# Top-k attention on Trainium2: a penalty moved to GpSimd and the programs of four engines put in another order

## The reference

```python
scores = jnp.einsum('bhnd,bhmd->bhnm', q, k) * DHEAD ** (-0.5)
kth = jax.lax.top_k(scores, TOPK)[0][..., -1:]
masked = jnp.where(scores >= kth, scores, jnp.finfo(scores.dtype).min)
attn = jax.nn.softmax(masked, axis=-1)
o = jnp.einsum('bhnm,bhmd->bhnd', attn, v)
```

## Time and profile before

| What | Value |
|---|---|
| Median of 3 runs | 5586.61 us (5582.31 to 5589.42) |
| The profiled execution, its own time | 5584.55 us |
| Its span, first to last instruction | 5582.5 us |
| Top-k stage, first to last hand-on (L667) | 139.2 to 3348.1 us |
| TensorE matmuls busy | 4367.2 us (78%) |
| VectorE busy | 4406.7 us (79%) |
| ScalarE busy | 4164.0 us (75%) |
| GpSimd busy | 1502.2 us (27%) |
| Mean granted TensorE clock | 0.832 of full speed |

### The profile page before, as it was taken

One profiled execution on the slowest core, in us unless ns is written; L12 is line 12 of the kernel. 1 busy time (PEld: TensorE's weight loads), 2 busy tenths in 40 slices (PEclk: granted clock), 3 DMA queues, 4 the chain that ended last, 5 costly groups with the idle time before them and its releaser, 6 DMA issues. The chain is left out here.

```text
span 5582.5 us, 114219 instructions
## 1 busy us (share of the span) xinstructions
PE 4367.2 (78%) x32459; PEld 2805.0 (50%) x32459; DVE 4406.7 (79%) x25684; ACT 4164.0 (75%) x6084; POOL 1502.2 (27%) x362
## 2 busy tenths in 40 slices
PE   7575677766777477677777678988999999999998
PEld 4443445544544244445544454445655655655655
DVE  4999999989999999999999993224777777777775
ACT  2786799988988589889998893433666766666664
POOL 0443444444544244444554440010000000000000
PEclk8777677777777677777777779989999999999999
DMA  5000000000000000000000001014010010010012
GB/s 198 6 17 14 7 17 17 9 14 17 16 8 16 5 16 17 15 7 17 17 7 17 16 16 44 8 40 158 22 29 21 22 30 21 21 30 21 22 30 86
DMA packets 79607, 154.88 MB, mean 28 GB/s; under 512 B 8120, under 2 KB 49464, under 8 KB 73528
## 3 DMA queue, kind: packets, MB, share of 16 engines
q1 hardware_dynamic: 78904, 146.72, 9.3%
HBM read 99.50 MB, written 47.19 MB: 26 GB/s over the span
## 5 line engine op out<-in xcount | busy, mean ns | idle before, releaser
L539 POOL TENSOR_TENSOR a_probs<-a_scores,a_probs 128x2304 f32<-128x2304 f32 x288 | 1460.3, 5090 | 1778.2 <-ACT a_probs L462 1778.2
L557 DVE MAX8 a_top<-a_scores 128x8 f32<-128x36 f32 x18432 | 1831.2, 180 | 46.4 <-ACT a_scores L446 45.7
L373 PE MATMUL a_ps_t<-ident,a_probs 128*128 128x128 f32 x5184 | 976.2, 326 | 702.5 <-ACT a_probs_t L457 570.8
L373 PEld LDWEIGHTS a_ps_t<-ident,a_probs 128*128 128x128 f32 x5184 | 675.5, 164 | 989.4 <-ACT a_probs_t L457 707.5
L1110 PE MATMUL b_ps_t<-ident,b_soft 128*128 128x128 f32 x5184 | 794.3, 286 | 97.9 <-ACT b_soft_t L1183 69.6
L462 ACT ACTIVATE a_probs<-a_scores,a_steep_kth 128x2304 f32<-128x2304 f32 x290 | 641.2, 2211 | 294.7 <-DVE a_minus_max L667 294.7
L1195 DVE TENSOR_SCALAR_CACHE_REDUCE b_soft<-b_ps_s 128x2304 f32<-128x2304 f32 x290 | 741.7, 2558 | 86.9 <-PE b_ps_s L1097 67.3
L1183 ACT ACTIVATE b_soft_t<-b_ps_t 128x512 f32<-128x512 f32 (+1 forms) x864 | 438.0, 525 | 473.2 <-PE b_ps_t L1110 472.5
L1110 PEld LDWEIGHTS b_ps_t<-ident,b_soft 128*128 128x128 f32 x5184 | 557.6, 142 | 450.8 <-issue 304.2
L457 ACT ACTIVATE a_probs_t<-a_ps_t 128x512 f32<-128x512 f32 (+1 forms) x1440 | 726.8, 545 | 20.7 <-PE a_ps_t L373 7.2
L1168 ACT ACTIVATE b_soft<-b_soft,b_minus_max 128x2304 f32<-128x2304 f32 x289 | 642.1, 2222 | 30.2 <-issue 16.8
(11 more groups left out here) (127 smaller groups left out, 4279.6 us busy)
## 6 DMA issues: line engine op xcount, KB each, us to landing
a_k_stack<-k_parts SPq DMA_DIRECT2D x72, 288.0 KB, 6.0
b_k_stack<-k_parts SPq DMA_DIRECT2D x72, 288.0 KB, 6.1
a_q_ring<-q_parts SPq DMA_DIRECT2D x294, 64.0 KB
b_q_ring<-q_parts SPq DMA_DIRECT2D x294, 64.0 KB
k_parts<-p_high SPq DMA_DIRECT2D x36, 256.0 KB, 2.1
k_parts<-p_rest SPq DMA_DIRECT2D x36, 256.0 KB, 2.2
q_parts<-p_high SPq DMA_DIRECT2D x36, 256.0 KB, 2.0
q_parts<-p_rest SPq DMA_DIRECT2D x36, 256.0 KB, 2.0
```

What stands on the lines that cost most here:

```text
L373: last = pe.transpose(ps_t[(NTG * s + g) % 2][:, P * m:P * m + P], probs[s % 2][:, P * (m0 + m):P * (m0 + m) + P], cst["ident"][:, :])
L539: pool.tensor_tensor(probs[u][:, :], scores_all[:, 2 * (p % 2) + u, :], probs[u][:, :], ALU.subtract).then_inc(masked_ready, 1)
L557: last = dve.max(top8[s // 2 % 2][:, s % 2, c, :], scores_all[:, s % 4, CHUNK * c:CHUNK * c + CHUNK])
```

## The change

GpSimd makes the first tile's penalty itself: a tensor_scalar writes 3e38 where the score is below the 64th value and 0 elsewhere, from a new small tile `kept_kth`, and its subtraction follows. ScalarE makes the second tile's penalty only, as the last step of its pair. ScalarE's pair begins with `keep_scores` of the pair two ahead, which now waits until GpSimd has read the slot. TensorE's order follows; `weigh` of the second tile's last groups and `add_quadrants` move into the next pair. On VectorE `select` comes ahead of all chunks of the next pair, the last part of it (`pick`) after chunk 23 and `hand_on` after chunk 47. TensorE's and ScalarE's loops run 7 times from pair 2 on, with pairs before and after written out; GpSimd's first head is written out.

```diff
@@ TensorE @@
+            def pair_step(p, h):
+                pair = h * HEAD_PAIRS + p
+                here, before, after = exists(pair), exists(pair - 1), exists(pair + 1)
+                if exists(pair + 2):
+                    score(p + 2, 0, h)
+                if before:
+                    for g in range(2, NTG):
+                        weigh(p - 1, 1, g, h)
+                if exists(pair + 2):
+                    score(p + 2, 1, h)
+                if here:
+                    for g in range(3):
+                        turn(p, 0, g, h)
+                if before:
+                    pe.wait_ge(parts_ready, pair)
+                if after:
+                    count_doubts(pair + 1)
+                if here:
+                    turn(p, 0, 3, h)
+                    turn(p, 0, 4, h)
+                if after:
+                    pe.wait_ge(any_ready, pair + 2)
+                if before:
+                    add_quadrants(pair - 1)
+                    pe.wait_ge(o_kept, pair)
+                if here:
...
+                    for g in range(NTG):
+                        weigh(p, 0, g, h)
+                    for g in range(3):
+                        turn(p, 1, g, h)
+                    weigh(p, 1, 0, h)
+                    turn(p, 1, 3, h)
+                    turn(p, 1, 4, h)
+                    weigh(p, 1, 1, h)
+
+            for p in range(-2, 2):
+                pair_step(p, 0)
+            with pe.Fori(0, HEADS - 1) as h:
+                for p in range(2, HEAD_PAIRS + 2):
+                    pair_step(p, h)
+            for p in range(2, HEAD_PAIRS + 1):
+                pair_step(p, HEADS - 1)
...
@@ ScalarE @@
+                if exists(pair - 2):
+                    act.wait_ge(masked_ready, tile - 3)
+                act.activation(scores_all[:, 2 * (p % 2) + u, :], ps_s[:, 0:N], ACT.Copy).then_inc(scores_kept, 1)
...
+                if second:
+                    keep_scores(p + 2, 0, h)
+                if here:
+                    exponentials(p, 0, h)
+                    keep_turned(p, 0, 0, h)
+                if before:
+                    keep_parts(pair - 1)
+                if here:
+                    keep_turned(p, 0, 1, h)
+                    keep_turned(p, 0, 2, h)
+                if after:
                     keep_any(pair + 1)
...
+                if second:
+                    keep_scores(p + 2, 1, h)
+                if here:
+                    keep_turned(p, 0, 3, h)
+                if before:
+                    finish(p - 1, h)
+                if here:
+                    keep_turned(p, 0, 4, h)
+                    exponentials(p, 1, h)
+                if second:
+                    guess_place(p + 2, 0, h)
+                if here:
+                    for g in range(4):
+                        keep_turned(p, 1, g, h)
+                if second:
+                    guess_place(p + 2, 1, h)
+                if here:
+                    keep_turned(p, 1, 4, h)
+                if after:
+                    penalty(p + 1, 1, h)
...
@@ GpSimd @@
+                if u == 0:
+                    if not first:
+                        wait_alone(pool, turned, pair * (2 * NTG) - NTG)
+                    wait_alone(pool, kth_ready, pair + 1)
+                    pool.tensor_scalar(probs[0][:, :], scores_all[:, 2 * parity, :], kept_kth[parity][:, 0:1], -LOWEST,
+                                       ALU.is_lt, ALU.mult).then_inc(first_penalty, 1)
+                    pool.wait_ge(first_penalty, pair + 1)
+                else:
+                    pool.wait_ge(penalty_ready, pair + 1)
+                pool.tensor_tensor(probs[u][:, :], scores_all[:, 2 * parity + u, :], probs[u][:, :],
+                                   ALU.subtract).then_inc(masked_ready, 1)
...
@@ VectorE @@
+                return found
+
+            def pick(found):
                 for u in range(2):
                     after(found[u])
...
                 dve.tensor_scalar(steep_kth[parity][:, :], kth[:, :], STEEP, None, ALU.mult)
+                dve.tensor_scalar(kept_kth[parity][:, :], kth[:, :], 1.0, None, ALU.mult)
...
+                found = select(pair - 1, top8[(p - 1) % 2]) if before else None
+
                 def between(c):
-                    if c == 7 and before:
-                        select(pair - 1, top8[(p - 1) % 2])
-                    if c == 19 and before:
+                    if c == 23 and before:
+                        pick(found)
+                    if c == 47 and before:
                         hand_on(pair - 1, (p - 1) % 2)
```

More of the change, by code:

```diff
@@ L303, in attention_top @@
         minus_max = [sb(f"minus_max{n}", [P, 2]) for n in range(2)]
+        kept_kth = [sb(f"kept_kth{n}", [P, 2]) for n in range(2)]
         above = sb("above", [P, 1])
@@ L321, in attention_top, with exists @@
         HEAD_PAIRS = B * PAIRS
+        def exists(pair):
+            return not isinstance(pair, int) or 0 <= pair < ALL_PAIRS
         block = ctx.enter_context(nc.Block())
@@ L403, in add_quadrants @@
                 last.then_inc(added, 1)
-            score(0, 0, 0, first=True)
-            for s in range(1, 5):
-                score(s, 0, s)
-            count_doubts(0)
-            with pe.Fori(0, HEADS) as h:
-                for p in range(HEAD_PAIRS):
-                    pair, tile = h * HEAD_PAIRS + p, h * HEAD_TILES + 2 * p
-                    s = 2 * p
-                    pe.wait_ge(probs_ready, tile + 1)
-                    turn(s, 0, tile)
-                    turn(s, 1, tile)
-                    score(s + 5, h, tile + 5)
+            def pair_step(p, h):
[24 more added lines that the diff above has]
+                if here:
@@ L452, in exponentials, with keep_turned @@
+            def exponentials(p, u, h):
+                ahead, of_head = divmod(p, HEAD_PAIRS)
+                act.wait_ge(masked_ready, h * HEAD_TILES + 2 * p + u + 1)
+                act.activation(probs[u][:, :], probs[u][:, :], ACT.Exp, scale=SCALE,
+                               bias=minus_max[p % 2][:, u:u + 1], accum_out=sums[:, 2 * of_head + u, cols(h + ahead, 1)]
                                ).then_inc(probs_ready, 1)
-            def keep_turned(s, g, tile):
+            def keep_turned(p, u, g, h):
@@ L487, in finish @@
+            def finish(p, h):
+                ahead, of_head = divmod(p, HEAD_PAIRS)
+                act.wait_ge(added, h * HEAD_PAIRS + p + 1)
+                act.activation(o_all[:, 2 * of_head:2 * of_head + 2, cols((h + ahead) * D, D)],
                                ps_o[:, O_COL:O_COL + 2 * D].rearrange("p (u d) -> p u d", d=D),
                                ACT.Copy).then_inc(o_kept, 1)
-            for s in range(4):
-                keep_scores(s, s)
-            for u in range(2):
-                guess_place(u, 0, 0)
@@ new lines, in pair_step @@
+            def pair_step(p, h):
+                pair = h * HEAD_PAIRS + p
+                here, before, after, second = exists(pair), exists(pair - 1), exists(pair + 1), exists(pair + 2)
+                if second:
[9 more added lines that the diff above has]
+                if after:
+                    keep_any(pair + 1)
+                if second:
[18 more added lines that the diff above has]
+                    penalty(p + 1, 1, h)
@@ L526, in _ @@
+            for p in range(-2, 2):
+                pair_step(p, 0)
+            with act.Fori(0, HEADS - 1) as h:
+                for p in range(2, HEAD_PAIRS + 2):
+                    pair_step(p, h)
+            for p in range(2, HEAD_PAIRS + 1):
+                pair_step(p, HEADS - 1)
         @block.gpsimd
```

165 lines of the change are left out of this document (55 added, 110 removed).

## The result

The changed kernel takes **6740.84 us** (median of 4 runs, 6737.73 to 6748.61), the kernel before 5585.26 us beside it (4 runs). The ratio is 1.207, with a 95% interval of 1.205 to 1.2091. Forecast were 5539 us and a range up to 5670, so the sign and the size were both wrong. The profiled execution took 6748.61 us, its span is 6746.8.

The account below looks back on a forecast made before the run. It took a ring through VectorE, ScalarE and GpSimd as the bound, 20.6 us a plain pair; 20.3 after the change, 0.34 less times 143, gave -48 us from 5584.55: 5537, plus 2.1, 5539 us; range 5470 to 5670.

Parts of the forecast that it names:

- The tensor_scalar (x): GpSimd's added 128x2304 tensor_scalar ahead of its first subtraction: taken as 2.8 us, costing nothing until about 4.
- a late GpSimd blocks select: First subtraction still runs when VectorE starts select, whose first operation must wait; decides from x = 4; 5724 us, chance 0.20.
- S + 16.2 + x: Start of the next select when GpSimd is late, S being this select's start; 21.6 us a pair with x = 5.4.
- The port: VectorE and GpSimd excluding each other on SBUF: GpSimd's second subtraction against select's last operands, taken to add zero.
- margin of 0.2: Second subtraction starts about S + 2.1, S being select's start; select reads its last two-input operands at S + 1.96.
- The failed margin: GpSimd's second subtraction gets in ahead of select's last operands: up to +700 us, above 6200, chance 0.04.
- The row of 0.29 us: Trace row: select's first operation took 0.29 us beside a GpSimd copy and ended with it; elsewhere it takes 0.17.
- VectorE's own pair: VectorE's work from one select start through chunks, pick, hand-on and prepare: 19.76 us if nothing is late.
- The recounts: 19 recounts in VectorE's top-k stage, 8.0 us each over a plain pair, 152 us together, kept unchanged.
- The rival of a slow TensorE: ScalarE's wait for TensorE sets the period: 20.8 us a pair if TensorE stays at low clock, 5608 us, chance 0.17.
- Its counterargument: At the low clock TensorE is almost always busy, and the mean of 0.75 says it always returned to 2.4 GHz.
- Loop-backs: Seven loop-backs of ScalarE, 2.56 us each, 17.9 together, left as they are, between -18 and +18.

Follow-up runs that it names:

- prices by themselves: Kernel before with a block in front timing GpSimd forms over 128x2304 alone, then eight small VectorE operations begun during GpSimd subtractions; the change's tensor_scalar took 8.04 us.
- x = 6.10: Changed kernel with GpSimd's tensor_scalar doing the comparison alone, the multiplication by 3e38 left out: 6465.6 us.
- x = 2.11: Changed kernel with GpSimd's tensor_scalar writing a constant by mult and add, the comparison left out: 5570.76 us.
- a pair of edits that each read as "no use": Kernel before with first penalty and first subtraction in two pieces, and a pair's finish moved behind the next first exponential: both 0.9947, finish alone 1.002, pieces alone 1.0022.

## Why the prediction was wrong

**The tensor_scalar (x): the step that failed first.** The prediction took 2.8 us and 2.7 to 5.4 as bounds. It is 8.04. The low end rested on a COPY as "the only wide one-input row"; the run with prices by themselves has 2.10 for the copy and 6.10 with one comparison, so the kind of operation mattered more than the number of inputs. The high end took the subtraction's rate as that of a slow instruction; with two operations the rate is 8.04 / 2304 = 3.49 ns a column, where the subtraction has 2.2. An upper bound had to stand above it: the only tensor_scalar in the trace, 602 ns for 128 columns, allowed for up to 4.7 ns a column, or 10.8 us, and was discounted as fixed cost on no row's evidence. The prediction's two estimates, 2.0 and 3.9 us, came from the Trainium skill, GPSIMD Engine Reference: 1.03 cycles per element stands under Performance versus the Vector engine, the 2.03 of compare bodies under Performance pitfalls for Q7 kernels and not where the prediction puts it. The measured 6.04 to 8.05 us disagree with both.

**The rival "a late GpSimd blocks select" was the mechanism,** with its price formula right. S + 16.2 + x with x = 8.04 is 24.24 a pair, (24.24 - 20.64) x 143 = 515, or 6100 us. The run with the second subtraction held back, in which only this block exists, took 6094.4, with pairs of 24.15 to 24.45. By the formula the block at x = 6.10 should be 1.94 shorter than at 8.04; `factor` was 1.88 shorter.

**The port: the step that failed second.** "I take zero" with a margin of 0.2 us was worked out for a `select` that starts on time. In that case the second subtraction starts when ScalarE's penalty ends, just behind `select`'s last operand. When the first subtraction is late, the second's penalty is already made, and the second follows 0.1 us behind the first, while `select` has only just got its first instruction through. Then `guess` is caught by the whole 5 us. The failed margin was priced at up to +700 and given one chance in twenty-five, as if it were independent of the first. It is not: **a late first subtraction brought the failed margin with it**, in 143 of 144 pairs with x = 8.04 and again in 143 with 6.10. It is 4.83 x 143 = 691 us, against 646 measured when it was taken away. The two rivals' prices add up: 515 + 691 = 1206 against the 1156 that came, and the range reached neither.

The row of 0.29 us was a trace of this block, and a 128x2 tile begun 1.31 us into a 5.03 us subtraction took 3.75. What the Trainium skill, SBUF — State Buffer, Who interferes with whom, says of it (one of the two engines is shut out for a whole instruction) agrees with these runs: each of the 143 long `factor` and 143 long `guess` records of the changed kernel ends within 0.1 us of the end of a subtraction. What was missing was to ask of each instruction of `select` what happens if its start moves.

**What held.** VectorE's own pair: forecast 19.76, found 19.86. The recounts: 8.0 over a plain pair before, and 36.8 against 28.82 after. With x = 2.11 the pair is 20.4 against a forecast of 20.3, and VectorE's idle time in front of the hand-on is 67.2 us in 122 waits, 0.55 each where 0.45 or none was forecast. The rival of a slow TensorE didn't come: with x = 2.11 its granted clock is 0.81 between 2000 and 3000 us, where it was 0.75. (Its counterargument was weaker than said: in one stretch before, 647 to 657 us, TensorE was granted 0.52 and busy 7.58 us of 10, not almost always.)

**What was mis-sized even so.** "Loop-backs: I leave 17.9 as it is (between -18 and +18)". With x = 2.11 ScalarE's 17.9 us are gone, but VectorE's own back edges stand in front of `select` in the new order, where the sum has nothing: 12.2 us in six waits. They also break the margin of 0.2, and each brings a whole block of 4.35 to 5.09 with it. All in all, with the first pair's block, these places cost 22 us more than before and not 0. The plain pairs gave some 0.23 each and not 0.34. So with the penalty that the prediction assumed, the stage gets 10 us shorter by its hand-ons (3199.3 against 3208.9), the one run is 19 us below those before, and not 48.

**What stays open.** Whether the new order pays with the port avoided altogether: by the prices above, `factor` and `guess` with one side in PSUM would not be blocked. It wasn't tried. It might only move the block: `beyond` (L645) and `select`'s two scalar_tensor_tensor instructions (L648) come 0.8 and 0.9 us behind `guess`'s end, while GpSimd would still be subtracting, and both kinds are blocked too (3.74 us at L139, 3.96 at L143). The blocks at VectorE's back edges were read from the trace of one run; no run holds the second subtraction back with x = 2.11.

## What to carry to other kernels

Before work is moved to GpSimd, look for the same operation with the same number of operations at a similar width: a copy, or a small tile whose time is taken for fixed cost, bounds nothing from above. When two engines shut each other out for a whole instruction, a margin between them holds only for the schedule for which it was computed; recompute it for every rival in which one engine is late and for every place where a loop goes back, and add the prices of rivals that cause one another. If one of two waits stands behind the other, neither edit alone gains, and a pair of edits that each read as "no use" may be the one that works.

## What the runs showed of the hardware that was not expected

GpSimd's tensor_scalar over 128x2304 has three prices in the run with prices by themselves: 2.11 us for mult and add with constants, 6.0 to 6.1 for one operation with a constant or a column, 8.0 for two of which the first is a comparison or a subtraction, each form run once. It is odd that one multiplication (6.04) takes three times as long as a multiplication and an addition (2.11); what chooses the fast form stays open. The block of VectorE counts as busy time in the profile: a busy share of 97% hid 9 us of standing still in each 28.8, and only the mean duration of a two-column tile gave it away. An accumulator output or one side in PSUM was enough to escape it.
